# Cross attention and expert layer on one core: score exponentials with an immediate factor instead of a factor read from a tile

## The chip, the cores and the metric

The kernel runs on one core of a Trainium2 chip. The metric is the device time of one execution in microseconds (us); the median of several executions is compared.

## What is computed

Eight batches of 512 tokens, width 512. The first layer is cross attention with 16 heads of 32; the second is an expert layer. Cut to what matters here:

```python
qh = (layernorm(x) @ Wq + bq)   # 16 heads of 32
kh, vh = ctx @ Wk + bk, ctx @ Wv + bv
sim = einsum('bnid,bnjd->bnij', qh, kh) * 32 ** -0.5
sim = where(~attention_mask[:, None, None, :], finfo.min, sim)
attn = softmax(sim, axis=-1)
x = x + (attn @ vh) @ Wo + bo
x = x + experts(layernorm(x))   # 8 experts, each takes its top 512 tokens
```

The mask has one value per batch and key. If a batch had no valid key at all, every score would be the same large negative number and the softmax would be uniform; the kernel must keep that case. With the inputs given, every key is valid.

## The kernel before

**Groups.** The work of attention is cut into 32 groups: a group is one batch and four heads, so a batch is four groups. For a group the kernel projects q and k (`proj`, lines 1888 to 1890, three matmuls per 128 rows of the width, since each float32 operand is split into a rounded part and a rest, called hi and lo). The projections leave PSUM twice: ScalarE writes the hi part with the bias (L1271), VectorE the lo part (L1480). SyncE stores both to memory (`keep_hi`, `keep_lo`) and loads them again as a stack of rows per head (`stack_hi`, `stack_lo`), so that one matmul of 97 or 99 rows gives the exact product of the split numbers, with further rows for the mask and the row maxima. The q weights and the q bias carry the factor -1/sqrt(32), so every score in PSUM has its sign turned.

**Two passes over the scores.** The first pass (`max`, 16 matmuls per group, L1906) has queries on the partitions. VectorE takes the minimum (L1495), which is the negative of the row maximum, and ScalarE forms exp(-(score) + minimum) with its sum (`sum`, L1294). The maxima are turned (`rows`, L1923) and written into the q stack by two small DMAs from GpSimd's queue. The second pass (`score`, 16 matmuls, L1938) has keys on the partitions, with the maximum already subtracted by the extra rows; ScalarE forms the exponential into one of ten buffers `p_ring` (L1306), and `att` (L1950) multiplies it by v. Here the exponential's factor is read from the tile `keep_scale`, one column per batch: -1 where a batch has a valid key, and 0 where it has none, so that all exponentials are 1 there.

**Where the factor comes from.** In the hand-written first steps VectorE computes the mask row (`mask`, L1444), and later (`any`, L1447 to L1451) a block of -1, the maximum of each mask row, and a diagonal of it; TensorE multiplies the two (`scale`, L1854) and VectorE copies the result (L1455).

**Once per batch.** The next batch's x is loaded, its statistics taken (L1399 to L1403), normalised (L1408), turned by TensorE (`turn`, L1848) and split: ScalarE copies the hi part (L1242), VectorE subtracts for the lo part (L1425). The context is split the same way (L1251, L1431), v projected (L899 to L901), and the output projected, added to x, normalised and routed (L1966 to L2000).

**What sets the order.** Up to the first six maxima of group 1 the order is written out in `first_steps`, and PSUM banks are handed out in turn by `take_bank`. From there a planner (`Plan.run`) simulates the five engines with the table `COST`: for each kind of step how long the engine is taken and after how long the result is seen. Each step has a due time `at` in units of groups, from tables of tuned numbers (`LAG`, `K_AT`, `Q_AT`, `MAX_AT`, `SPAN`). Of the steps that could start on an engine within 0.0426 us of the earliest it takes the one with the earliest due time. The order that comes out is the order in which each engine's program is written; banks are given in the same simulation. At run time only semaphores count. After group 31 the kernel chooses the tokens of the experts and runs the expert layer, which the planner doesn't touch.

Line numbers above 1230 and below 1350 are ScalarE's program, 1390 to 1800 VectorE's, above 1840 TensorE's.

## Time and profile before

| | us |
|---|---|
| Median of 3 runs | 1653.18 (1652.41 to 1653.51) |
| Span of the profiled execution | 1648.1 |
| Median less span, what lies around it | 5.1 |

The profiled execution shows a span of 1648.1 us from the first to the last instruction; its own time outside the span isn't recorded, so the 5.1 us are the median less the span. Engines are called PE (TensorE; PEld are its weight loads), ACT (ScalarE), DVE (VectorE), POOL (GpSimd) and SP (SyncE). The page's second part cuts the span into 40 slices of 41.2 us and gives the busy tenths of each:

```profile
PE   7999999999999999999885999999999999999998
DVE  7687978879788797887736688675554555454553
ACT  5899898998989989899863223222222223232321
PEclk9999999999999999999988999999999999999999
```

Attention fills the first 21 slices, the choice of tokens the next one, and the experts the rest.

### The profile page before, as it was taken

The numbers are of one execution on the slowest core, as the hardware profiler recorded it, in microseconds if no ns is written. First come the engines' busy times: TensorE is split into PE (matmuls) and PEld (weight loads), VectorE is DVE, ScalarE is ACT, GpSimd is POOL, SyncE is SP. The second block draws the span as 40 slices with busy tenths as digits, with TensorE's granted clock in tenths as the row PEclk, the third lists the DMA queues.
The fourth block names the chain that finished last, engine by engine and source line by source line (L and its number), as shares of the span: only waits on it lengthen the run. The fifth ranks groups of instructions, "written<-read, shape, count | busy, mean of one in ns | idle before, by whom it ended". The sixth has DMA issues, their size and how long they took to land.

```text
span 1648.1 us, 22236 instructions
## 1 busy us (share of the span) xinstructions
PE 1581.2 (96%) x7826; PEld 1164.5 (71%) x7826; DVE 1118.8 (68%) x1976; ACT 979.2 (59%) x2119; POOL 302.8 (18%) x396
## 2 busy tenths in 40 slices
PE   7999999999999999999885999999999999999998
PEld 5657666676666766667543777888888888888886
DVE  7687978879788797887736688675554555454553
ACT  5899898998989989899863223222222223232321
POOL 6220321302213032130300201002020202020100
PEclk9999999999999999999988999999999999999999
DMA  5543644636446364463601433416253525333340
GB/s 180 178 137 105 204 143 136 187 106 204 142 136 187 106 203 142 138 185 110 205 36 65 129 102 96 142 52 186 77 160 103 160 78 159 103 103 134 99 131 26
DMA packets 131271, 217.26 MB, mean 132 GB/s; under 512 B 17117, under 2 KB 51057, under 8 KB 131161
## 3 DMA queue, kind: packets, MB, share of 16 engines
q1 hardware_dynamic: 114520, 173.23, 33.4%
q0 software_dynamic: 16640, 42.61, 9.9%
q8 instruction: 63, 1.03, 0.3%
q14 instruction: 48, 0.39, 0.1%
HBM read 157.45 MB, written 57.82 MB: 131 GB/s over the span
## 4 chain that ended last, share of the span: by engine, by line
PE 72%; DVE 13%; ACT 9%; DMA 3%; issue 2%; POOL 0%; SPq 0%; ACTq 0%; DVEq 0%; POOLq 0%
PE ps_gen L899 9%; PE ps_gen L900 9%; PE ps_gen L901 9%; PE ps_gen L2107 7%; PE ps_gen L2108 7%; PE ps_gen L2109 7%; PE ps_att L1950 5%; PE ps_gen L1938 4%; PE ps_gen L1906 4%; ACT ps_gen L1294 4%; ACT p_ring L1306 4%; DVE nmax L1495 4%; PE ps_gen L1888 2%; PE ps_gen L1889 1%; PE ps_gen L1890 1%
## 5 line engine op out<-in xcount | busy, mean ns | idle before, releaser
L1495 DVE TENSOR_REDUCE nmax<-ps_gen 128x1 f32<-128x512 f32 x512 | 329.6, 684 | 60.5 <-PE ps_gen L1906 59.8
L1294 ACT ACTIVATE ps_gen<-ps_gen,nmax 128x512 f32<-128x512 f32 x512 | 350.2, 695 | 24.5 <-DVE nmax L1495 24.1
L1306 ACT ACTIVATE p_ring<-ps_gen,keep_scale 128x512 f32<-128x512 f32 x512 | 343.7, 716 | 32.6 <-PE ps_gen L1938 28.7
L1368 ACT ACTIVATE gel<-ps_gen,b_cols 128x512 f32<-128x512 f32 x128 | 88.4, 690 | 446.3 <-PE ps_gen L901 434.1
L1770 DVE TENSOR_TENSOR gel_lo<-gel,gel_hi 128x512 fp32r<-128x512 f32 x126 | 87.3, 693 | 269.3 <-ACT gel_hi L1369 265.0
L899 PE MATMUL ps_gen<-hT_hi,w_hi 128*128 128x512 f32 x504 | 199.2, 395 | 0.0
L2107 PE MATMUL ps_gen<-w_hi,gel_hi 128*128 128x512 f32 x504 | 198.0, 393 | 0.0
L901 PE MATMUL ps_gen<-hT_hi,w_lo 128*128 128x512 f32 x504 | 196.4, 390 | 0.0
L2109 PE MATMUL ps_gen<-w_hi,gel_lo 128*128 128x512 f32 x504 | 196.4, 390 | 0.0
L900 PE MATMUL ps_gen<-hT_lo,w_hi 128*128 128x512 f32 x504 | 196.3, 390 | 0.0
L2108 PE MATMUL ps_gen<-w_lo,gel_hi 128*128 128x512 f32 x504 | 196.2, 389 | 0.0
L1938 PE MATMUL ps_gen<-qst,kst 99*128 99x512 f32 x512 | 192.2, 423 | 3.2 <-ACT p_ring L1306 2.3
L1906 PE MATMUL ps_gen<-kst,qst 97*128 97x512 f32 x512 | 184.3, 415 | 8.1 <-issue 6.0
L1216 POOL DMA_INDIRECT out_x<-y_out,idx x28 | 48.7, 1739 | 508.9 <-ACT y_out L1388 502.5
L1938 PEld LDWEIGHTS ps_gen<-qst,kst 99*128 99x128 f32 x512 | 93.8, 190 | 62.8 <-issue 33.5
L1906 PEld LDWEIGHTS ps_gen<-kst,qst 97*128 97x128 f32 x512 | 96.6, 189 | 58.4 <-issue 26.9
L1950 PE MATMUL ps_att<-p_ring,v_sb 128*32 128x512 f32 x1024 | 127.6, 617 | 4.2 <-ACT p_ring L1306 3.9
L1294 ACT ACTIVATION_READ_ACCUMULATOR ps_gen<-ps_gen,nmax 128x1 f32 x512 | 122.8, 240 | 0.0
L901 PEld LDWEIGHTS ps_gen<-hT_hi,w_lo 128*128 128x128 f32 x504 | 94.6, 188 | 20.2
L2109 PEld LDWEIGHTS ps_gen<-w_hi,gel_lo 128*128 128x128 f32 x504 | 94.6, 188 | 19.7
L2107 PEld LDWEIGHTS ps_gen<-w_hi,gel_hi 128*128 128x128 f32 x504 | 94.8, 188 | 19.3
L899 PEld LDWEIGHTS ps_gen<-hT_hi,w_hi 128*128 128x128 f32 x504 | 94.6, 188 | 19.3 <-issue 0.2
(233 smaller groups left out, 2699.9 us busy)
## 6 DMA issues: line engine op xcount, KB each, us to landing
w_raw<-in_L_ffn_W SPq DMA_DIRECT2D x128, 512.0 KB, 5.2
kst<-qk_rows SPq DMA_DIRECT2D x93, 256.0 KB, 3.9
qst<-qk_rows SPq DMA_DIRECT2D x93, 256.0 KB, 3.7
x_in<-in_x POOLq DMA_DIRECT2D x60, 256.0 KB, 4.0
out_x<-x_in SPq DMA_DIRECT2D x32, 256.0 KB, 2.3
qk_rows<-kT_hi SPq DMA_DIRECT2D x31, 256.0 KB, 2.2
qk_rows<-kT_lo SPq DMA_DIRECT2D x31, 256.0 KB, 3.5
qk_rows<-qT_hi SPq DMA_DIRECT2D x31, 256.0 KB, 2.0
```

Source lines behind the costliest of these rows:

```text
L899: e.matmul(psum, lhsT=wh, rhs=mh, start=(i == 0), stop=False)
L900: e.matmul(psum, lhsT=wh, rhs=ml, start=False, stop=False)
L901: last = e.matmul(psum, lhsT=wl, rhs=mh, start=False, stop=(i == n - 1))
L1294: e.activation(psum[:, :], psum[:, :], ACT.Exp, bias=nmax[g % 2][:, c], scale=-1.0, accum_out=den[g % 2][:, c]).then_inc(drained_sem("max" ...
L1306: e.activation(p_ring[n % NP_][:, :], ps("score", g, kt, h)[:, :], ACT.Exp, scale=keep_scale[:, b:b + 1]).then_inc(drained_sem("score", g, ...
L1495: e.tensor_reduce(nmax[g % 2][:, h * TB + t:h * TB + t + 1], ps("max", g, h, t)[:, :], AX.X, ALU.min).then_inc(s_min, 1)
L1906: e.matmul(ps("max", g, h, t)[:, :], lhsT=qst[k][0:ROWS_MAX, h, t * P:(t + 1) * P], rhs=kst[k][0:ROWS_MAX, h, :], start=True, stop=True).t ...
L1938: e.matmul(ps("score", g, kt, h)[:, :], lhsT=kst[k][0:ROWS_ALL, h, kt * P:(kt + 1) * P], rhs=qst[k][0:ROWS_ALL, h, :], start=True, stop=Tr ...
L1950: last = e.matmul(ps_att[h * DH:(h + 1) * DH, :], lhsT=v_sb[:, kt, (c4 * HG + h) * DH:(c4 * HG + h + 1) * DH], rhs=p_ring[((g * KT + kt) * ...
L2107: e.matmul(ps_y[tt], lhsT=gh, rhs=wh, start=(j == 0), stop=False)
L2108: e.matmul(ps_y[tt], lhsT=gh, rhs=wl, start=False, stop=False)
L2109: return e.matmul(ps_y[tt], lhsT=gl, rhs=wh, start=False, stop=(j == NF - 1))
```

## The change

The exponential of the second pass takes the immediate factor -1. The case of a batch without a valid key is carried by the operands instead: `keep`, 1 or 0 per batch, is multiplied into x as it leaves PSUM after the turn (hi and lo), and into the q bias (`bias_q`, one column per batch and group), so q is zero there; and the mask row of such a batch is multiplied by the batch's own maximum and so becomes zero. The memset, the maximum and the diagonal move into the `mask` step at the head of VectorE's queue, the matmul and the copy of the factors to just ahead of the first turn. The cost table gets the new times for `score` and `turn` on ScalarE and `turn_lo` on VectorE; the due times stay.

```diff
--- before.py
+++ after.py
@@ -283,6 +283,7 @@
     a.add("picks")
     a.stats(0, 0)
     a.add("csplit", 0, 0)
+    a.with_bank("scale")
     for t in range(TB):
         if t + 1 < TB:
             a.add("csplit", 0, t + 1)
@@ -322,7 +323,6 @@
     for t in range(TB):
         a.max_of(0, 0, t)
     a.flush()
-    a.add("any")
     for w, h in (("k", 1), ("q", 2)):
         for i in range(DC):
             a.project(w, 1, i)
@@ -336,7 +336,6 @@
     for t in range(TB):
         a.max_of(0, 3, t)
     a.flush()
-    a.with_bank("scale")
     a.with_bank("v", 0, 1)
     a.max_rows(0)
     a.flush()
@@ -355,12 +354,12 @@
     "pe": {"proj": (0.700, 0.90), "max": (0.235, 0.43), "rows": (0.109, 0.31), "rden": (0.436, 0.63), "score": (0.235, 0.43),
            "att": (1.975, 2.03), "v": (2.78, 2.98), "turn": (0.436, 0.63), "outa": (1.395, 1.60), "osum": (1.650, 1.85),
            "out": (1.395, 1.60), "route": (0.436, 0.63), "logits": (0.405, 0.52), "back": (0.109, 0.31)},
-    "act": {"proj": (0.585, 0.73), "sum": (0.662, 0.82), "rows": (0.174, 0.30), "score": (0.570, 0.72), "osplit": (0.613, 0.79),
-            "csplit": (0.520, 0.66), "turn": (0.477, 0.64), "out": (0.570, 0.70), "logits": (0.157, 0.31), "route": (0.477, 0.64),
+    "act": {"proj": (0.585, 0.73), "sum": (0.662, 0.82), "rows": (0.174, 0.30), "score": (0.477, 0.63), "osplit": (0.613, 0.79),
+            "csplit": (0.520, 0.66), "turn": (0.570, 0.73), "out": (0.570, 0.70), "logits": (0.157, 0.31), "route": (0.477, 0.64),
             "choice_exp": (0.136, 0.26), "wsplit": (0.585, 0.72)},
     "dve": {"proj_lo": (0.658, 0.78), "max": (0.600, 0.72), "rows_lo": (0.313, 0.32), "recip": (0.160, 0.30), "rden": (0.597, 0.72),
             "divide": (0.592, 0.72), "osplit_lo": (0.659, 0.78), "v": (0.570, 0.72), "csplit_lo": (0.600, 0.72),
-            "stats": (1.020, 1.10), "norm": (0.453, 0.57), "turn_lo": (0.598, 0.72), "outa": (0.600, 0.72), "out": (1.750, 1.80),
+            "stats": (1.020, 1.10), "norm": (0.453, 0.57), "turn_lo": (0.660, 0.78), "outa": (0.600, 0.72), "out": (1.750, 1.80),
             "x1_norm": (0.453, 0.57), "route": (0.602, 0.72), "back": (0.300, 0.35), "choice_max": (0.330, 0.41),
             "choice": (0.540, 0.60), "wsplit": (0.660, 0.78), "tables": (0.500, 0.60)},
     "pool": {"rows_lo": (1.050, 3.20), "recip": (0.560, 0.66), "load": (0.550, 4.00), "load_wo": (0.550, 3.30),
@@ -616,7 +615,8 @@
         bs_b = sb(p1, "bs_b", [P, E])
         bias_cols = sb(p1, "bias_cols", [P, 3 * DC])
         half = sb(p1, "half", [P, 1])
-        keep_scale = sb(p1, "keep_scale", [P, B])
+        keep = sb(p1, "keep", [P, B])
+        bias_q = sb(p1, "bias_q", [P, B, DC])
         nmax = [sb(p1, f"nmax{i}", [P, HG * TB]) for i in range(2)]
         den = [sb(p1, f"den{i}", [P, HG * TB]) for i in range(2)]
         rden = sb(p1, "rden", [P, HG * TB])
@@ -625,7 +625,7 @@
         rstd = [sb(p1, f"rstd{i}", [P, 1]) for i in range(NSTAT)]
         rt_max = sb(p1, "rt_max", [P, TB])
         rt_sum = sb(p1, "rt_sum", [P, TB])
-        mask_any = sb(p1, "mask_any", [B, 1])
+        mask_any = sb(p1, "mask_any", [B, 2])
         mask_diag = hnT[0:B, 3, 0:B]
         ones_b = hnT[0:B, 0, :]
         mask_u8 = hnT[0:B, 1, :].bitcast(U8)
@@ -715,6 +715,7 @@
         s_w_hi, s_w_lo = sem("s_w_hi"), sem("s_w_lo")
         s_picks = sem("s_picks")
         s_mask, s_mask_store, s_any = sem("s_mask"), sem("s_mask_store"), sem("s_any")
+        s_bias_q = sem("s_bias_q")
         s_proj_hi = {w: sem(f"s_proj_hi_{w}") for w in "qk"}
         s_kept_hi, s_kept_lo = {w: sem(f"s_kept_hi_{w}") for w in "qk"}, {w: sem(f"s_kept_lo_{w}") for w in "qk"}
         s_stack_hi = {w: [sem(f"s_stack_hi_{w}{i}") for i in range(NST)] for w in "qk"}
@@ -842,6 +843,10 @@
 
         def stack_of(w, g):
             return (qst if w == "q" else kst)[g % NST]
+
+        def bias_of(w, g):
+            b, c4 = divmod(g, GB)
+            return bias_q[:, b, c4:c4 + 1] if w == "q" else bias_cols[:, DC + c4:DC + c4 + 1]
 
         def kept(w, g, part):
             return qk_rows["qk".index(w), g % 2, part]
@@ -1239,8 +1244,9 @@
                     on.wait_ge(*full("turn", b, t))
                     if b > 0:
                         on.wait_ge(*full("proj", "q", b * GB - 1))
+                    on.wait_ge(*drained("scale"))
                     e.activation(xT[0][:, :, t * P:(t + 1) * P], ps("turn", b, t)[:, :].rearrange("p (c t) -> p c t", c=DC),
-                                 ACT.Copy).then_inc(s_turn_hi, 1)
+                                 ACT.Copy, scale=keep[:, b:b + 1]).then_inc(s_turn_hi, 1)
 
                 elif kind == "csplit":
                     b, c = at
@@ -1260,8 +1266,7 @@
 
                 elif kind == "proj" and at[2] == DC - 1:
                     w, g, _ = at
-                    n = ("q", "k").index(w) * DC + g % GB
-                    on.wait_ge(*drained("bias"))
+                    on.wait_ge(*(drained("bias") if w == "k" else (s_bias_q, 1)))
                     on.wait_ge(*full("proj", w, g))
                     if g == 1:
                         on.wait_ge(*full("pick", w, HG - 1))
@@ -1269,7 +1274,7 @@
                         on.wait_ge(s_kept_hi[w], 16 * (g - 1))
                         on.wait_ge(*drained("proj", w, g - 1))
                     e.activation(qk[w, "hi"][:, :], ps("proj", w, g)[:, :], ACT.Identity,
-                                 bias=bias_cols[:, n:n + 1]).then_inc(s_proj_hi[w], 1)
+                                 bias=bias_of(w, g)).then_inc(s_proj_hi[w], 1)
 
                 elif kind == "pick" and at[1] % 2 == 0:
                     w, h = at
@@ -1296,15 +1301,13 @@
 
                 elif kind == "score":
                     g, kt, h = at
-                    b = g // GB
                     n = (g * KT + kt) * HG + h
-                    on.wait_ge(*drained("scale"))
                     on.wait_ge(s_w_lo, W_NO["o"])
                     on.wait_ge(*full("score", g, kt, h))
                     if n >= NP_:
                         on.wait_ge(s_av, (n - NP_) // (PAIR * HG) + 1)
                     e.activation(p_ring[n % NP_][:, :], ps("score", g, kt, h)[:, :], ACT.Exp,
-                                 scale=keep_scale[:, b:b + 1]).then_inc(drained_sem("score", g, kt, h), 1)
+                                 scale=-1.0).then_inc(drained_sem("score", g, kt, h), 1)
 
                 elif kind == "osplit":
                     g, = at
@@ -1422,8 +1425,9 @@
                     hi, lo = xT
                     cols = slice(t * P, (t + 1) * P)
                     on.wait_ge(s_turn_hi, b * TB + t + 1)
-                    e.tensor_tensor(lo[:, :, cols], ps("turn", b, t)[:, :].rearrange("p (c t) -> p c t", c=DC),
-                                    raw(hi[:, :, cols]), ALU.subtract).then_inc(drained_sem("turn", b, t), 1)
+                    on.wait_ge(*drained("scale"))
+                    e.scalar_tensor_tensor(lo[:, :, cols], ps("turn", b, t)[:, :].rearrange("p (c t) -> p c t", c=DC), keep[:, b:b + 1],
+                                           raw(hi[:, :, cols]), ALU.mult, ALU.subtract).then_inc(drained_sem("turn", b, t), 1)
 
                 elif kind == "csplit_lo":
                     b, c = at
@@ -1441,23 +1445,27 @@
 
                 elif kind == "mask":
                     on.wait_ge(s_mask_in, 16)
-                    e.tensor_scalar(mask_neg, mask_u8, 1.0, -MASKED, ALU.subtract, ALU.mult).then_inc(s_mask, 1)
-
-                elif kind == "any":
-                    e.memset(ones_b, -1.0).then_inc(s_any, 1)
-                    e.reduce_max(mask_any[:, :], mask_u8, AX.X).then_inc(s_any, 1)
+                    e.memset(ones_b, 1.0).then_inc(s_any, 1)
+                    e.reduce_max(mask_any[:, 0:1], mask_u8, AX.X).then_inc(s_any, 1)
                     on.wait_ge(s_any, 2)
+                    e.tensor_scalar(mask_any[:, 1:2], mask_any[:, 0:1], -MASKED, None, ALU.mult).then_inc(s_any, 1)
                     on.wait_ge(s_ident, 2)
                     e.tensor_scalar(mask_diag, ident[0:B, 0:B], mask_any[:, 0:1], None, ALU.mult).then_inc(s_any, 1)
+                    on.wait_ge(s_any, 3)
+                    e.tensor_scalar(mask_neg, mask_u8, 1.0, mask_any[:, 1:2], ALU.subtract, ALU.mult).then_inc(s_mask, 1)
 
                 elif kind == "scale":
                     on.wait_ge(*full("scale"))
-                    e.tensor_copy(keep_scale[:, :], ps("scale")[:, 0:B]).then_inc(drained_sem("scale"), 1)
+                    e.tensor_copy(keep[:, :], ps("scale")[:, 0:B]).then_inc(drained_sem("scale"), 1)
 
                 elif kind == "bias":
                     on.wait_ge(*full("bias"))
                     e.tensor_copy(bias_cols[:, DC:3 * DC], ps("bias")[:, DC:3 * DC])
                     e.tensor_scalar(bias_cols[:, 0:DC], ps("bias")[:, 0:DC], -SCALE, None, ALU.mult).then_inc(drained_sem("bias"), 1)
+                    on.wait_ge(*drained("bias"))
+                    on.wait_ge(*drained("scale"))
+                    e.tensor_tensor(bias_q[:, :, :], bias_cols[:, 0:DC].rearrange("p (b c) -> p b c", b=1).to_broadcast([P, B, DC]),
+                                    keep[:, :].rearrange("p (b c) -> p b c", c=1).to_broadcast([P, B, DC]), ALU.mult).then_inc(s_bias_q, 1)
 
                 elif kind == "wsplit":
                     w, c = at
@@ -1470,14 +1478,13 @@
 
                 elif kind == "proj_lo":
                     w, g = at
-                    n = ("q", "k").index(w) * DC + g % GB
                     on.wait_ge(s_proj_hi[w], g + 1)
-                    on.wait_ge(*drained("bias"))
+                    on.wait_ge(*(drained("bias") if w == "k" else (s_bias_q, 1)))
                     if g == 1:
                         on.wait_ge(*full("pick", w, HG - 1))
                     if g > 1:
                         on.wait_ge(s_kept_lo[w], 16 * (g - 1))
-                    e.scalar_tensor_tensor(qk[w, "lo"][:, :], ps("proj", w, g)[:, :], bias_cols[:, n:n + 1],
+                    e.scalar_tensor_tensor(qk[w, "lo"][:, :], ps("proj", w, g)[:, :], bias_of(w, g),
                                            raw(qk[w, "hi"][:, :]), ALU.add, ALU.subtract).then_inc(drained_sem("proj", w, g), 1)
 
                 elif kind == "pick" and at[1] % 2 == 1:
@@ -1850,7 +1857,7 @@
 
                 elif kind == "scale":
                     on.wait_ge(*free("scale"))
-                    on.wait_ge(s_any, 3)
+                    on.wait_ge(s_any, 4)
                     e.matmul(ps("scale")[:, 0:B], lhsT=ones_b, rhs=mask_diag, start=True, stop=True).then_inc(full_sem("scale"), 1)
 
                 elif kind == "bias":
```

## Rows read from the trace of the kernel before

**Rows 1.** The page, part 1: busy us, share of the span, instructions.
```profile
PE 1581.2 (96%) x7826; PEld 1164.5 (71%) x7826; DVE 1118.8 (68%) x1976; ACT 979.2 (59%) x2119; POOL 302.8 (18%) x396
```

**Rows 2.** Busy time by group of attention: length, engines' busy time, granted clock, DMA.
```profile
77.50:106.40 28.90, 26.06 (x127) 13.97 (x127) 24.84 (x50) 28.21 (x67) 13.22 (x17) 0.95 0.64 189
...
153.90:180.80 26.90, 26.90 (x153) 18.80 (x152) 23.54 (x46) 21.44 (x49) 4.67 (x8) 1.00 0.59 186
180.80:208.60 27.80, 26.78 (x149) 17.09 (x148) 27.25 (x63) 27.24 (x65) 10.82 (x18) 1.00 0.71 201
208.60:232.30 23.70, 23.48 (x119) 15.60 (x116) 18.18 (x31) 22.21 (x53) 6.45 (x7) 1.00 0.45 134
...
826.60:850.20 23.60, 19.60 (x93) 11.47 (x89) 12.77 (x21) 18.36 (x42) 1.58 (x3) 0.86 0.05 20
```

**Rows 3.** Chain of waits, 180.8 to 208.6: start, length, what (first, last).
```profile
180.60 0.60 DVE hnT L1542
...
208.05 0.61 DVE nmax L1495
```

**Rows 4.** Chain of waits, 208.6 to 260 us.
```profile
208.68 0.78 ACT ps_gen L1294 x2
...
219.30 1.16 ACT p_ring L1306 x2
...
226.84 0.66 PE ps_gen L1930 x4
```

**Rows 5.** Waits 150 to 790 us: who, after whom, us, times, longest.
```profile
PEld ps_att L1950 <- ACT p_ring L1306: 5.5, 17, 0.4
...
PEld ps_gen L1938 <- ACT p_ring L1306: 3.7, 13, 0.4
PEld ps_gen L1906 <- ACT ps_gen L1294: 3.2, 12, 0.3
PEld ps_gen L1966 <- ACT ps_gen L1294: 2.9, 6, 0.5
...
PEld ps_gen L1930 <- ACT ps_gen L1294: 2.6, 6, 0.5
...
PE ps_gen L1906 <- issue: 1.1, 3, 0.7
PE ps_gen L1966 <- ACT ps_gen L1294: 1.0, 6, 0.2
```

**Rows 6.** Instructions by line and shape: count, busy us, mean ns, idle before.
```profile
L1306 ACT ACTIVATE p_ring<-ps_gen,keep_scale 128x512 f32<-128x512 f32 x512 | 343.7, 716 | 32.6 <-PE ps_gen L1938 28.7 <-PE ps_att L1950 3.7
...
L1242 ACT ACTIVATE xT_hi<-ps_gen 128x512 fp32r<-128x512 f32 x32 | 19.2, 615 | 2.6 <-PE ps_gen L1848 2.4
...
L1480 DVE SCALAR_TENSOR_TENSOR qT_lo<-ps_gen,bias_cols,qT_hi 128x512 fp32r<-128x512 f32 x32 | 24.0, 749 | 28.2 <-ACT qT_hi L1271 27.9
...
L1425 DVE TENSOR_TENSOR xT_lo<-ps_gen,xT_hi 128x512 fp32r<-128x512 f32 x32 | 20.9, 683 | 0.0
```

**Rows 7.** Chain of waits, 0 to 110 us.
```profile
54.68 1.74 ACT p_ring L1306 x3
...
63.78 5.58 DMA qk_rows<-qT_hi
...
98.24 0.97 ACT xT_hi L1242 x2
```

**Rows 8.** Chain of waits, 800 to 880 us: the last four scores.
```profile
863.95 2.43 ACT p_ring L1306 x4
```

**Rows 9.** Timeline of the start: start, length, engine, line, [idle before <-releaser].
```profile
8.28 0.69 DVE L1399 BATCH_NORM_STATS2 stat<-x_in 128x6 f32<-128x512 f32 x1 [0.63 <-DMA x_in<-in_x]
...
31.64 2.58 DVE L1451 TENSOR_SCALAR hnT<-ident,mask_any 8x8 f32<-8x8 f32 x1
...
32.38 1.81 POOL L1097 MEMSET qst<- 32x2048 f32 x1
...
41.92 0.50 PE L899 MATMUL ps_gen<-wv_hi,cT_hi 128*128 128x512 f32 x1 [0.28 <-ACT ps_gen L1294]
```

## The prediction, made before the changed kernel ran

> **What bounds the kernel now.** I read the page's first section, then the busy time of each engine over single attention groups, then the chain of waits, and last the waits by engine. Over the whole execution TensorE is busy 96% of the span and ScalarE 59% [rows 1]. That average hides three stages: a start of some 52 us, attention up to about 870 us, and the experts, which the change doesn't touch. The question is who limits attention.
>
> Attention runs in batches of four groups, and the groups are not alike [rows 2]. In the group from 153.9 us TensorE is busy for all of its 26.9 us. In the next one, from 180.8, VectorE is busy for 27.25 of 27.8 us and ScalarE for 27.24, while TensorE loses a microsecond: this is where the next batch is normalised and turned. After it TensorE is again at 23.48 of 23.7 us. The first batch (77.5 to 106.4) and the last (826.6 to 850.2) are looser for TensorE, and its granted clock dips to 0.95 and 0.86 there.
>
> The chain of waits says the same in another way. From 180.6 to 208.7 us it stays on VectorE alone [rows 3]. Then it lies on ScalarE from 208.68 to 226.8 us, and from 226.84 on TensorE [rows 4]. So ScalarE, whose work gets cheaper, holds the end for some 18 us of each batch, with TensorE close behind it. Last, the waits from 150 to 790 us: TensorE's weight loads stood idle after ScalarE for 5.5 + 3.7 + 3.2 + 2.9 + 2.6 = 17.9 us, and its matmuls for 1.0 us [rows 5]. That stretch has six full batches.
>
> **The change, part by part.** The profiled execution has a span of 1648.1 us; the median of the runs is 1653.18, so 5.1 us lie around the span. I leave those alone and give the result as a median.
>
> *A score exponential.* It reads the factor from a tile now, and takes 716 ns; a copy from PSUM with an immediate factor takes 615 ns [rows 6]. What counts is the step from one to the next in the chain: 1.16 us for two scores, so 0.58 [rows 4], against 0.97 for two turns, 0.485 [rows 7]. I take 0.095 us off each of 512 scores, 48.6 us of ScalarE's time. Nothing in the trace shows an exponential without any operand from a tile; the price lies between 0 and the 101 ns of the durations, and I take the one nearest, the copy. Per batch that is 64 x 0.095 = 6.1 us, and most of it is worth nothing, since ScalarE isn't last there.
>
> *What of it reaches the end, between the first and the last batch.* The chain's ScalarE stretch holds 14 scores: 14 x 0.095 = 1.33 us, in six batches 8.0 us. But TensorE is idle only 0.2 us in that group, so as soon as ScalarE is faster it is the bound. The lower end is what TensorE's matmuls waited for ScalarE, 1.0 us; the upper end adds the weight loads, 18.9 us. I take 6, the chain's value cut a little because TensorE is so near.
>
> *The turns.* Four times a batch ScalarE's copy of the turned x gets a factor from a tile (+0.095 each) and VectorE's subtraction becomes the three-operand form with a factor from a tile: 683 becomes 749 ns [rows 6], +0.066. The four subtractions lie in the group where the chain is VectorE throughout [rows 3], so nothing covers them: 6 x 4 x 0.066 = +1.6 us. The four copies lie beside the relief of 16 scores there.
>
> *First batch.* The chain from 54.7 to 99.2 us carries 18 scores and three turns [rows 7]: -18 x 0.095 + 3 x 0.095 = -1.4 us. **Last batches.** From 797 us on it carries 14 scores, the last four in one row of 2.43 us [rows 8]: -1.3 us.
>
> *The start.* New on VectorE, ahead of the first statistics, are a memset, a maximum over the mask rows, a tiny product and the diagonal. They, and the copy of the factors, are covered by the wait for x, which still ends at 8.28 after 0.63 us of idleness [rows 9]; without that cover they would cost some 1.3 us. The step at risk is the diagonal: in the old place it took 2.58 us for 8x8 elements, and ended at 34.22, when GpSimd's memset ended at 34.19 [rows 9]. GpSimd is filling the picking matrices where the step goes. I take +0.2 from a range of 0 to 2.6. The Trainium skill (SBUF — State Buffer, section "Who interferes with whom") says that VectorE and GpSimd share one pair of ports as an exclusive lock, and the second to issue stands until the first is done. By it the diagonal and the mask row would both stand behind GpSimd's fill, and the start would cost about 1 us more than my sum has. The trace agrees for the old place.
>
> The product of bias and factors adds a small VectorE instruction (about 0.2 us with its wait) on the path to the first projections, and one dearer copy with three dearer subtractions there adds 0.09 + 3 x 0.066 = 0.3. In return the old step is gone from between the first projections (0 to 2.58 us, mostly under the wait for the k rows), and a bank is no longer taken before the v tiles, where TensorE stood 0.28 us for ScalarE [rows 9]. I take -0.5. The start is +0.2 + 0.2 + 0.3 - 0.5 = +0.2 us. The matmul for the factors only moves; no DMA is added, and in the start the SyncE queue keeps its order: it issues the mask's store behind all the first loads, when the row has long been there.
>
> *The sum:* -6.0 + 1.6 - 1.4 - 1.3 + 0.2 = -6.9 us; 1653.2 - 6.9 = 1646.3, and I give 1646. A difference under 0.2% (3.3 us) can't be told from none by a measurement of this kernel.
>
> **The planner.** Orders on all queues and the banks are computed from the cost table, so three new costs reshuffle them from batch 0 on, with due times that stay. This is a mechanism of its own that the sum can't contain; it makes the two rivals at the ends.
>
> **The rivals.** (1) *VectorE and TensorE hold the pace.* The gain behind 208 us vanishes because TensorE was ready to be last, and only the first and last batches gain: 1.6 - 1.4 - 1.3 + 0.2 = -0.9, 1652.3. For it speaks TensorE's 99% in that group; against it the waits behind ScalarE.
> (2) *Much more.* A less loaded ScalarE lets the planner close all waits behind it: -18.9 + 1.6 - 1.4 - 1.3 + 0.2 = -19.8, 1633.4. For it: every dip of the granted clock (0.95, 0.86) stands where TensorE waited, so they would go as well. Against it: weight loads' waits are partly hidden behind matmuls.
> (3) *Slower: the q and k rows come late.* Rows are stored, and loaded again as a stack, and the first maximum of the next group waits for them. In the first batch the store alone took 5.58 us and stood in the chain [rows 7]. In the steady part this is just in time: three waits, 1.1 us, the longest 0.7 [rows 5]. If the reshuffle puts a projection behind scores that now come ready earlier, each of 24 groups may wait 0.7 us: +16.8 - 6.9 = +9.9, 1663. It decides against the forecast from (6.9 + 3.3) / 24 = 0.43 us a group.
> (4) *The exponential isn't cheaper without the tile.* Then only the additions are left: +1.6 + 0.3 + 0.2 = +2.1, 1655.3. Nothing speaks for it but that no row shows such an exponential.
>
> **How the numbers follow.** Forecast 0.45; (1) 0.20; (2) 0.13; (3) 0.18; (4) 0.04. Faster: 0.45 + 0.13 = 0.58. Same: 0.20 + 0.04 = 0.24. Slower: 0.18. The range goes from close to rival 2 to where a mild form of rival 3 ends, 1634 to 1657.
>
> **What would show it.** Scores at about 615 ns and stepping 0.485 us; turns at 716 and 749 ns; the group with the turns still 27.8 us or a little more, its chain VectorE; the group after it about 1 us shorter, TensorE's waits on ScalarE down from 18.9 to under 10 us; the first statistics for x tile 2 still near 8.3 us. I would be wrong if the four groups kept their lengths, if scores kept 716 ns, or if first maxima waited on landings.

## The result, and the profile after

The changed kernel takes 1671.13 us (median of 4 runs, 1668.95 to 1675.18), the kernel before 1653.35 (4 runs): a ratio of 1.0106, 95% interval 1.0087 to 1.0125. It is 17.8 us slower where 7 us less had been forecast, and lies outside the range. The span of the profiled execution grew from 1648.1 to 1667.1 us.

First what went as foreseen. The page, part 1, and the groups by line and shape [rows 1, 6 before]:

```profile
PE 1589.0 (95%) x7826; PEld 1171.2 (70%) x7826; DVE 1118.8 (67%) x1978; ACT 943.8 (57%) x2119; POOL 298.1 (18%) x396
...
L1309 ACT ACTIVATE p_ring<-ps_gen 128x512 f32<-128x512 f32 x512 | 289.7, 611 | 45.9 <-PE ps_gen L1945 38.6 <-PE ps_att L1957 3.3
...
L1429 DVE SCALAR_TENSOR_TENSOR xT_lo<-ps_gen,keep,xT_hi 128x512 fp32r<-128x512 f32 x32 | 22.3, 739 | 0.0
L1248 ACT ACTIVATE xT_hi<-ps_gen,keep 128x512 fp32r<-128x512 f32 x32 | 20.3, 674 | 12.3 <-PE ps_gen L1855 12.3
```

A score exponential takes 611 instead of 716 ns, and ScalarE is busy for 35.4 us less (943.8 instead of 979.2). The sums of the first pass, which did not change, are 21 ns shorter too (674 instead of 695). The turns take 739 (683 before) and 674 ns (615 before). From one score to the next, the chain of waits has 0.485 us, as forecast (0.58 before, [rows 4]):

```profile
264.74 0.97 ACT p_ring L1309 x2
```

Yet TensorE, with the same 7826 matmuls, is busy for 7.8 us more.

The time of single groups, in the columns of [rows 2] (a window begins with the first score of its group):

```profile
157.80:184.70 26.90, 26.90 (x155) 18.53 (x153) 23.10 (x47) 20.68 (x49) 5.23 (x9) 1.00 0.61 186
184.70:214.30 29.60, 27.99 (x145) 18.40 (x144) 26.66 (x60) 26.40 (x64) 8.93 (x17) 0.88 0.65 175
214.30:239.80 25.50, 24.75 (x122) 16.77 (x121) 20.31 (x34) 23.22 (x59) 7.06 (x8) 1.00 0.58 172
239.80:263.90 24.10, 23.91 (x120) 16.52 (x119) 14.23 (x25) 20.28 (x51) 1.58 (x3) 1.00 0.18 56
...
291.80:319.30 27.50, 25.64 (x146) 16.86 (x145) 26.18 (x60) 25.90 (x64) 8.95 (x17) 1.00 0.68 192
```

The group with the turns takes 29.6 us in one batch and 27.5 in the next, and so on alternately; the granted clock is 0.88 in the long one. The group after it, which the forecast had a microsecond shorter than its 23.7 us, takes 25.5. Only in the first of the four is an engine, TensorE, busy throughout. In the next two TensorE stands idle for 1.6 and 0.75 us, and no other engine fills the group either. The waits of TensorE's matmuls and weight loads from 150 to 790 us (columns of [rows 5]):

```profile
PE ps_gen L1913 <- ACT ps_gen L1299: 8.9, 9, 1.4
PE ps_gen L1973 <- ACT ps_gen L1299: 4.5, 6, 0.8
PE ps_gen L1988 <- DVE x_in L1411: 2.5, 3, 1.0
...
PEld ps_gen L1913 <- ACT ps_gen L1299: 13.3, 17, 1.6
PEld ps_gen L1945 <- ACT p_ring L1309: 9.1, 32, 0.4
```

TensorE waits for ScalarE longer than before, although each score left ScalarE a tenth of a microsecond of room: the matmuls for 8.9 + 4.5 us behind the sums, where they had 1.0 [rows 5]. The timeline around the first of these waits (start, length, engine, line, in brackets the idle time before and its releaser):

```profile
185.44 0.59 ACT L1309 ACTIVATE p_ring<-ps_gen 128x512 f32<-128x512 f32 x1
...
186.02 0.66 ACT L1299 ACTIVATE ps_gen<-ps_gen,nmax 128x512 f32<-128x512 f32 x1
...
186.70 1.14 ACT L1257 ACTIVATE cT_hi<-x_in 128x512 fp32r<-128x512 f32 x2
...
187.74 0.65 ACT L1299 ACTIVATE ps_gen<-ps_gen,nmax 128x512 f32<-128x512 f32 x1
...
188.56 0.50 PE L1913 MATMUL ps_gen<-kst,qst 97*128 97x512 f32 x1 [1.38 <-ACT ps_gen L1299]
```

Two copies of the next context (L1257) stand ahead of a sum in ScalarE's queue, and a maximum waits for the bank that this sum frees. The copies are no dearer than before (639 ns on average, 655 before); they stand elsewhere. A little later the granted clock falls. Two windows of the same group, columns as above:

```profile
184.70:190.00 5.30, 3.92 (x23) 2.39 (x22) 4.50 (x10) 5.24 (x13) 2.19 (x4) 1.00 0.47 157
190.00:196.80 6.80, 6.57 (x22) 4.13 (x23) 5.88 (x13) 5.89 (x16) 1.07 (x2) 0.50 0.73 218
```

TensorE was busy for 3.92 of 5.3 us with a clock of 1.00, and then for 6.8 us the granted clock is 0.50, 1.2 GHz instead of 2.4. Such stretches stand at 190.0, 401.7 and 613.3 us, in every second batch; before there was none between 150 and 790 us.

### The profile page after: what moved, and what is told of

Read it like the earlier page. It is cut to its first block, busy times and chain, and to the rows that moved or that the text cites. A ratio compares the mean times of both kernels' runs of the same rounds, so it can differ in the third digit from the quotient of the medians.

```text
span 1667.1 us, 22244 instructions
## 1 busy us (share of the span) xinstructions
PE 1589.0 (95%) x7826; PEld 1171.2 (70%) x7826; DVE 1118.8 (67%) x1978; ACT 943.8 (57%) x2119; POOL 298.1 (18%) x396
## 3 DMA queue, kind: packets, MB, share of 16 engines
q8 instruction: 63, 1.03, 0.3%
## 4 chain that ended last, share of the span: by engine, by line
PE 73%; DVE 12%; ACT 8%; DMA 4%; issue 2%; POOL 0%; SPq 0%; DVEq 0%; POOLq 0%; ACTq 0%
PE ps_gen L904 8%; PE ps_gen L906 8%; PE ps_gen L905 8%; PE ps_gen L2114 7%; PE ps_gen L2116 7%; PE ps_gen L2115 7%; PE ps_att L1957 5%; PE ps_gen L1945 5%; PE ps_gen L1913 4%; ACT ps_gen L1299 4%; DVE nmax L1502 3%; ACT p_ring L1309 2%; PE ps_gen L1973 2%; PE ps_gen L1895 1%; PE ps_gen L1896 1%
## 5 line engine op out<-in xcount | busy, mean ns | idle before, releaser
L1299 ACT ACTIVATE ps_gen<-ps_gen,nmax 128x512 f32<-128x512 f32 x512 | 342.9, 674 | 44.9 <-DVE nmax L1502 42.7
L1309 ACT ACTIVATE p_ring<-ps_gen 128x512 f32<-128x512 f32 x512 | 289.7, 611 | 45.9 <-PE ps_gen L1945 38.6
L1913 PE MATMUL ps_gen<-kst,qst 97*128 97x512 f32 x512 | 179.1, 419 | 17.5 <-ACT ps_gen L1299 10.3
L1299 ACT ACTIVATION_READ_ACCUMULATOR ps_gen<-ps_gen,nmax 128x1 f32 x512 | 112.1, 219 | 0.0
```

The lines of the kernel that those rows point to most:

```text
L1299: e.activation(psum[:, :], psum[:, :], ACT.Exp, bias=nmax[g % 2][:, c], scale=-1.0, accum_out=den[g % 2][:, c]).then_inc(drained_sem("max" ...
L1309: e.activation(p_ring[n % NP_][:, :], ps("score", g, kt, h)[:, :], ACT.Exp, scale=-1.0).then_inc(drained_sem("score", g, kt, h), 1)
L1913: e.matmul(ps("max", g, h, t)[:, :], lhsT=qst[k][0:ROWS_MAX, h, t * P:(t + 1) * P], rhs=kst[k][0:ROWS_MAX, h, :], start=True, stop=True).t ...
```

## The experiments

**Theory A**: the sum over the instructions is right, and the loss is the order of the queues, which the planner computes from the three changed costs. **Rival B**: the order is no worse than the old one, and the changed instructions cost more than counted (the turns on VectorE's path, the copy of the factors, the start). A second rival came with the results: the order is bad because a certain entry of the table is wrong, and a truer one would mend it.

**Old costs, all changed instructions.**

```diff
-    "act": ... "score": (0.477,0.63) ... "turn": (0.570,0.73)
+    "act": ... "score": (0.570,0.72) ... "turn": (0.477,0.64)
-    "dve": ... "turn_lo": (0.660, 0.78)
+    "dve": ... "turn_lo": (0.598, 0.72)
```

> The changed kernel with the three old entries of the cost table, so that all queues keep the order of the kernel before, and only the instructions and the start are new. Theory A (the new order is the loss, the instructions gain): about 1646 us, my forecast's sum, 1640 to 1651. Rival B (the dearer turns and the new start cost more than cheaper exponentials give, in any order): 1660 to 1672, near the changed kernel. Rival C (neither counts for much, the half clock stretches are chance): near 1653 with or without them.

Measured: 1646.13 us (5 runs), ratio 0.9960 (0.9946 to 0.9974). The forecast's sum was 1646.3. The planner writes every planned step of this kernel in the same place as in the kernel before. The groups, in the columns of [rows 2]:

```profile
153.00:179.90 26.90, 26.90 (x153) 18.86 (x152) 23.76 (x46) 20.52 (x49) 4.38 (x8) 1.00 0.57 186
179.90:207.90 28.00, 26.48 (x149) 17.14 (x148) 27.17 (x62) 26.79 (x64) 10.92 (x18) 1.00 0.69 206
207.90:230.80 22.90, 22.90 (x118) 15.49 (x115) 17.90 (x31) 21.05 (x53) 6.42 (x7) 1.00 0.39 130
230.80:255.10 24.30, 24.30 (x124) 16.93 (x123) 14.98 (x25) 22.70 (x56) 1.60 (x3) 1.00 0.33 90
```

The group with the turns takes 28.0 us (27.8 before), the next one 22.9 (23.7), and TensorE is busy in the whole of it. Of the waits from 150 to 790 us, the largest that is left behind ScalarE, and the longest of a matmul:

```profile
PEld ps_gen L1973 <- ACT ps_gen L1299: 2.4, 6, 0.4
...
PE ps_gen L1913 <- issue: 0.8, 2, 0.6
```

No stretch of lower clock stands between 150 and 790 us. Theory A holds: between this kernel and the changed one lie 25 us, and only the order differs, with the PSUM banks that go with it.

**New costs, all old instructions** (the reverse edit in the kernel before).

> The kernel before, with the three new entries of the cost table and nothing else: the changed kernel's order with the old instructions. Theory A: slower than the changed kernel, since the exponentials keep their 716 ns: 1672 to 1685 us. Rival B: near 1653, since none of the new instructions is there. Rival C: 1650 to 1660.

Measured: 1687.36 us, 1.0202 (1.0181 to 1.0223). This is theory A again, 2 us above its range, and no rival's. Both kernels have the same planned order. It costs the old instructions 33 us, the new ones 25.

**Which entry is it?** The changed kernel with the two turn entries of the table old, and with the score entry old:

```diff
-"turn": (0.570,0.73) ... "turn_lo": (0.660, 0.78)      # first
+"turn": (0.477,0.64) ... "turn_lo": (0.598, 0.72)
-"score": (0.477,0.63)                                  # second
+"score": (0.570,0.72)
```

> The changed kernel with the old entries for the turns alone, and the new one for the score. If the score's entry makes the bad order, the time stays at 1668 to 1675 us. If the turns' entries make it, the time falls to about 1646 to 1653.

> The changed kernel with the old entry for the score and the new ones for the turns: the reverse of the run in which the turns' entries were old. Sharp theory A: the plan's own end is 832.6 us, worse than with all three entries new (824.0), so about 1660 to 1680. Rival D: the turns' entries are four small steps in a batch, so near the changed kernel in the old order: 1645 to 1650.

Measured: 1674.61 us, 1.0125 (1.0099 to 1.0150), and 1683.41, 1.0172 (1.0149 to 1.0196). Each time is near the upper end of what was expected or above it (1668 to 1675, 1660 to 1680). Either change alone, the score entry's or the turn entries', is enough to lose the gain, and together (1671.1) they cost no more than either alone. These are not two effects that add up.

**Is it the size of the entry?** The kernel before, its score entry smaller by 10 ns and nothing else; and the changed kernel with a score entry of 0.460.

```diff
-"score": (0.570, 0.72)      # kernel before
+"score": (0.560, 0.713)
-"score": (0.477, 0.63)      # changed kernel
+"score": (0.460, 0.613)
```

> The kernel before with one number changed: the planner's entry for the score is 0.560 and 0.713 us in place of 0.570 and 0.72, ten nanoseconds less. Theory A in its sharp form (the due times fit one cost table exactly, and any other entry scatters the order): the plan's own end goes from 820.6 to 834.5 us, so the time should rise by about 14 us or more, to 1667 to 1690. Rival D (it was the size of the correction that mattered, scores that really come much earlier overtaking the maxima): ten nanoseconds change next to nothing, 1650 to 1657 us.

> The changed kernel with the score's entry at 0.460 and 0.613 us, 17 ns under what it takes. The plan's own end is 822.5 us, its batch 103.2, against 824.0 and 103.6 for the changed kernel. If the plan's end ranks orders, 1666 to 1671 us. If the loss comes from orders that are tight by wrong costs, this one, with an entry that is too low, should be no better than the changed kernel: 1671 or above.

Measured: 1706.03 us, 1.0310 (1.0277 to 1.0344), and 1667.52, 1.0074 (1.0048 to 1.0099). Ten nanoseconds in one entry cost 50 us, 16 more than the upper end expected. The entry that is 17 ns too low gave 1667.5 us beside 1671.1 with the measured one, so a truer entry doesn't mend the order, and the second rival is out. What waits there, from 160 to 820 us:

```profile
PE ps_gen L1906 <- issue: 16.5, 11, 2.9
```

These are the first maxima that wait for rows to land: rival 3 of the prediction, in a kernel whose table differs by one digit. In the changed kernel this wait does not appear; with the entry of 0.460 it comes to 3.8 us in five waits.

**The immediate factor alone**, in the kernel before, its order and its table kept (it leaves out the case of a batch without a valid key):

```diff
-ACT.Exp, scale=keep_scale[:, b:b + 1]
+ACT.Exp, scale=-1.0
```

> The kernel before, old order, whose score exponential takes the immediate factor -1, and nothing else is changed: the case of a batch without a valid key isn't handled in this kernel. It gives the exponentials' gain without the dearer turns and the new start. Theory A: 1.5 to 3 us faster than the changed kernel in the old order, about 1643 to 1645 us. Rival B: also clearly under 1653, but 15 us or more under the changed kernel in the old order. If the exponential were no cheaper for the path: 1653.

**Plain turns** in the old order (the changed kernel, old costs, `keep` not multiplied into x; the same case is left out):

```diff
-ACT.Copy, scale=keep[:, b:b + 1]
+ACT.Copy
-e.scalar_tensor_tensor(lo, ps, keep[:, b:b + 1], raw(hi), ALU.mult, ALU.subtract)
+e.tensor_tensor(lo, ps, raw(hi), ALU.subtract)
```

> The changed kernel in the old order, with plain turns: ScalarE's copy without the factor and VectorE's two-operand subtraction, so the case of a batch without a valid key isn't handled in this kernel. My forecast's term for the turns, 24 x 0.066 us plus 0.3 at the start: 1.9 us less than with the dear turns, about 1644 us. If ScalarE covers them or VectorE has room there: no difference, 1646.

Measured: 1648.33 us, 0.9967 (0.9957 to 0.9976), and 1646.71, 0.9960 (0.9946 to 0.9974). In the first the exponential takes this much (groups by line, shape kept apart):

```profile
L1306 ACT ACTIVATE p_ring<-ps_gen 128x512 f32<-128x512 f32 x512 | 291.5, 602 | 45.7 <-PE ps_gen L1938 38.5 <-PE ps_att L1950 4.0
```

The immediate factor brings 5.6 us by itself. The 1643 to 1645 us expected of it were missed: it is no faster than all changes together in the same order (1646.1). With the dearer turns taken away nothing more is gained either, 1646.7. In both profiled executions one first maximum comes late:

```profile
513.52 0.47 PE L1906 MATMUL ps_gen<-kst,qst 97*128 97x512 f32 x1 [1.15 <-issue]
```

```profile
512.58 0.47 PE L1913 MATMUL ps_gen<-kst,qst 97*128 97x512 f32 x1 [1.23 <-issue]
```

The first line is from the kernel before with the immediate factor, the second from the plain turns. Each makes its batch about a microsecond longer (103.05 and 103.17 us beside 102.1 to 102.2), and the clock did not fall behind it.

**New due times for the new table.** All due times were searched again, from two starts, for the earliest end in the planner's own reckoning: 796.3 and 803.4 us, against 824.0 for the changed kernel and 820.6 for the one before.

```diff
-K_AT = ((0.17737, 0.32917), (-0.06676, 0.27306), (0.03391, 0.12332), (-0.36248, 0.0798))
+K_AT = ((0.35915, 0.39022), (-0.13871, 0.11178), (-0.45119, 0.37669), (-0.05366, 0.45826))
...
```

> The changed kernel with its new cost entries and due times sought anew for them, by random steps that keep whatever made the plan's own end earlier: it is 796.3 us in place of 824.0, the batch 99.6 in place of 103.6. If the plan's end is what the chip follows (theory A: due times and costs have to fit each other), about 28 us less than the changed kernel: 1640 to 1648 us. If the plan's model leaves out what decides on the chip, an order pressed hard against the model gains less than half of that: 1655 to 1670.

> The same with another start of the search, the plan's end at 803.4 us, its batch 100.4. If the chip follows the plan: 7 us later than the other one, 1647 to 1655 us. If the model leaves out what decides, their order on the chip may be the reverse, both above 1655.

Measured: 1661.48 us (10 runs, from 1654.6 to 1668.4, a wider spread than the other kernels'), 1.0048 (1.0029 to 1.0067), and 1712.62, 1.0360 (1.0335 to 1.0385). The chip doesn't follow the plan's end: a gain under half of the 28 us for the first, a loss of 41 us against the changed kernel for the second. The waits of the second, from 160 to 820 us:

```profile
PE ps_gen L1975 <- DVE x_in L1398: 29.4, 6, 5.1
PE ps_gen L1932 <- DMA qst<-by_row: 15.2, 10, 2.6
```

In the second, TensorE waits 29.4 us for normalised x whose slot an output store still holds (L1398), and 15.2 us for the rows of maxima. So a plan that is shorter by the table isn't a faster kernel, and these waits are for transfers: that is the theory tested last.

**One wait by hand.** The changed kernel's order, with six steps moved after the planner has run: in batches 2 to 7 the sum stands ahead of the two copies of the context (first), or the sum and the two scores behind it (second).

```diff
+    act = a.order["act"]
+    for b in range(2, B):
+        i = act.index(("csplit", b, 0))
+        act[i:i + 3] = [act[i + 2], act[i], act[i + 1]]      # first
+        act[i:i + 5] = act[i + 2:i + 5] + act[i:i + 2]       # second
```

> The changed kernel and its order, but in batches 2 to 7 ScalarE's queue has one sum ahead of two copies of the context instead of behind them (six places, nothing else moves). In the changed kernel TensorE waits there 1.38 us, for the bank that this sum frees, and its clock falls to 1.2 GHz for 6.8 us in every second batch. Theory A, the order of single steps costs through such pauses and the clock falls because of them: the pause shrinks by two copies (1.14 us) to about 0.3, the half-clock stretches of 190, 402 and 613 us go, and the time is 1671 - 20.5/2 - 3 to 6 x 1.0 = 1655 to 1659. Theory B, the clock falls for another reason: pauses shrink but the stretches stay, 1665 to 1668. Theory C, the pause only moves (the context loads or the copies are late next, VectorE is last in this group): 1671, the group keeps its 29.6 us.

> As the last one, but the two copies of the context stand behind the sum and behind the two scores that follow it (batches 2 to 7), about as in the order of before. With the sum alone ahead of them, TensorE's 1.38 us were split into 0.34 us behind the sum and 1.03 us behind a score, the copies being late either way, and the clock fell in every batch instead of every second. Theory A, ScalarE's queue at this place is the cause and the copies can wait: both waits go, no half-clock stretch is left between 150 and 790 us, the turn group takes 27.0 instead of 27.5 to 29.7 us, and the time is 1671 - 6 x 1.0 - 3 x 2.2 = 1655 to 1660. Theory B, the wait moves on once more, to VectorE's lo parts, the loads of x behind them and the normalised x: a wait of 1 us or more of TensorE for x_in or hnT appears, and the time is 1670 to 1685.

Measured: 1681.18 us, 1.0167 (1.0149 to 1.0184), and 1689.00, 1.0210 (1.0193 to 1.0227): each slower than the last, the first above all three of its theories, the second 4 us above its theory B, whose sign, a wait for hnT, is there. The same place in the first, in a later batch, and then in the second (timelines):

```profile
293.45 0.49 PE L1918 MATMUL ps_gen<-kst,qst 97*128 97x512 f32 x1 [0.34 <-ACT ps_gen L1304]
294.98 0.49 PE L1950 MATMUL ps_gen<-qst,kst 99*128 99x512 f32 x1 [1.03 <-ACT p_ring L1314]
```

```profile
299.41 0.65 PE L2004 MATMUL ps_gen<-hnT,ws_sb 128*32 128x128 f32 x8 [2.43 <-DVE hnT L1554]
```

The 1.38 us turned into 0.34 + 1.03, behind the score that the copies now delay, and then into 2.43 us, because VectorE's queue has the lo parts of the same copies ahead of a copy (hnT) that TensorE needs.

**Both queues together.** As the second, and VectorE's two lo parts also stand behind what TensorE waited for:

```diff
+        dve = a.order["dve"]
+        i = dve.index(("csplit_lo", b, 0))
+        dve[i:i + 5] = dve[i + 2:i + 5] + dve[i:i + 2]
```

> As the last one (ScalarE's two context copies behind a sum and two scores), and VectorE's two lo parts of them stand behind a turned row block (hnT), a logits block and a maximum instead of ahead of them. In the last kernel TensorE waited 2.43 us for hnT behind these lo parts. Theory A, the two queues have to be moved together and then the wait is gone: no matmul waits longer than 0.8 us in the turn group, the stretches of half clock there vanish, the turn group takes 27 to 28 us and the time is 1655 to 1662. Theory B, the copies themselves are needed early, because the loads of x wait for them (the slots are shared): the statistics and the normalised x of the same group come later, TensorE waits for x_in, and the time stays at 1675 to 1690.

Measured: 1672.23 us, 1.0128 (1.0109 to 1.0147). The wait for hnT is gone (waits 150 to 790 us), and one behind a score is back:

```profile
PE ps_gen L1954 <- ACT p_ring L1318: 6.0, 6, 1.0
...
PE ps_gen L2008 <- DVE hnT L1558: 1.3, 5, 0.3
```

Against the second kernel some 15 us came back, against the changed one nothing. Neither theory had it quite: the two queues do belong together, but the pause of a microsecond returned at the next score. By hand this order wasn't mended.

**Due times searched against late landings.** The changed kernel, all due times searched again from two starts, this time for the mean end over the table's landing times and three sets of longer ones. The edit has the form of the retuned kernels' above.

> The changed kernel with all due times searched anew, as the two retuned kernels, but for the mean end over four sets of landing times of the transfers (the table's, and stores, reloads, row writes and loads 0.6 to 1.2 us longer, in part and all together). The first retuned kernels ended at 796 and 803 us by the table but lost 1.5 to 11 us per batch on the chip to waits for landings. This plan ends at 803 by the table and at 814 with all transfers longer; the order of before gives 821 and 852 in the same reckoning. Theory A, what the earlier plans missed were landings: about 102 us per batch at most, 1635 to 1646. Theory B, pauses of TensorE from other causes and the clock that falls after them decide, which no due time knows of: above 1650, with stretches of half clock between 150 and 790 us.

> As the last one, from another start of the search: 801 us by the table, 816 with all transfers longer. The same expectations: theory A 1635 to 1646, theory B above 1650. Two plans of nearly equal end also show how far apart such plans fall on the chip: the two earlier ones fell 51 us apart; if landings were the reason these should lie within 10 us of each other.

Measured: 1636.37 us (5 runs), 0.9905 (0.9885 to 0.9924), and 1645.78 (6 runs), 0.9955 (0.9940 to 0.9970). All that TensorE's matmuls still waited for in the first, from 150 to 790 us:

```profile
PE ps_gen L1994 <- ACT ps_gen L1286: 3.0, 6, 0.5
PE ps_gen L1932 <- DMA qst<-by_row: 2.1, 3, 0.8
PE ps_gen L1882 <- ACT ps_gen L1286: 2.0, 6, 0.3
```

No stretch of lower clock stands there in the first. It is faster than both kernels of this case, and than the old order with the new instructions; a batch takes 101.6 us on the chip and 100.6 by its plan, where the earlier retuned ones took 103.8 against 99.8, and 111.5 against 100.4. The second is just inside theory A's range, but shows theory B's signs: 103.5 us against 100.2, with three short stretches at 1.2 GHz and a pause of 1.7 us behind a sum. The two lie 9 us apart, within the 10 expected. In the first only 2.1 us of waits for landings are left, where the second of the earlier plans had 15.2 + 29.4. So late landings explain much of that plan's loss, and not all of what plans miss. That searching against them is what makes a plan better isn't shown by two plans of each kind, since each search also moved everything else. Both plans end later by the table than the first retuned one (803 and 801 against 796 us), and are 25 and 16 us faster on the chip. How much the old instructions would gain with such due times wasn't tried.

All kernels side by side. "Plan" is the planner's own end; "batch" is a sixth of the time from the first score of group 4 to that of group 28; "half" is the time at 1.2 GHz in between. The plans of the three orders moved by hand end at 824.0 before the move.

| kernel | instructions | table: score, turns | plan | batch, us | half, us | median, us |
|---|---|---|---|---|---|---|
| before | old | old, old | 820.6 | 102.9 | 0 | 1653.4 |
| e5_before_immediate | factor only | old, old | 820.6 | 102.3 | 0 | 1648.3 |
| e1_old_costs | new | old, old | 820.6 | 102.2 | 0 | 1646.1 |
| e8_plain_turns | new, plain turns | old, old | 820.6 | 102.5 | 0 | 1646.7 |
| after | new | new, new | 824.0 | 105.8 | 20 | 1671.1 |
| e2_new_costs_only | old | new, new | 824.0 | 109.2 | 41 | 1687.4 |
| e4_turn_costs_old | new | new, old | 823.8 | 106.6 | 24 | 1674.6 |
| e3_score_cost_old | new | old, new | 832.6 | 107.4 | 7 | 1683.4 |
| e6_score_cost_560 | old | 0.560, old | 834.5 | 111.8 | 27 | 1706.0 |
| e9_score_cost_460 | new | 0.460, new | 822.5 | 104.9 | 7 | 1667.5 |
| e7_retuned_a | new | new, new; due times | 796.3 | 103.8 | 3 | 1661.5 |
| e7_retuned_b | new | new, new; due times | 803.4 | 111.5 | 31 | 1712.6 |
| e10_sum_first | new | new, new; by hand | - | 108.4 | 48 | 1681.2 |
| e11_copies_later | new | new, new; by hand | - | 109.5 | 58 | 1689.0 |
| e12_both_later | new | new, new; by hand | - | 106.4 | 24 | 1672.2 |
| e13_robust_a | new | new, new; due times | 802.9 | 101.6 | 0 | 1636.4 |
| e13_robust_b | new | new, new; due times | 801.1 | 103.5 | 10 | 1645.8 |

As long as the due times stay, the plan's end puts the kernels with the new instructions in their measured order but for 0.2 us (820.6, 822.5, 823.8, 824.0, 832.6), though not to scale: 3.4 us of plan were 25 on the chip. Between different due times it doesn't rank them.

## Why the prediction was wrong

**The step that failed** is the paragraph on the planner, and with it rival 3's chance of 0.18. I wrote that three new costs reshuffle every queue and that the sum can't contain this, and then gave the sum 0.45 all the same, as if the new order would on average be as good as the old. So the sum has this term at nothing, and it measured 25.0 us with the new instructions (1671.1 against 1646.1) and 33.4 with the old ones. The old order goes with due times tuned for its table; of five other tables here (after, e3, e4, e6, e9) each gave a longer batch and a slower kernel, by 12 to 50 us against the kernel before. Seen from there the likeliest case was a loss, of a size that no row of before could bound.

**Where the 25 us went**, between e1_old_costs and the changed kernel (spans 1642.0 and 1667.1): up to the first score of group 4, 4.8 us (153.0 to 157.8); the six batches behind it 21.5 us; the end -1.2. Of the 4.8 us, 1.7 stand ahead of the first score of all (51.2 and 52.9 us), in steps whose order is the same in both: there the second tile of x landed at 5.57 and at 7.33 us. One batch of each without any stretch of lower clock, the sums over its four groups, first of the changed kernel (263.9 to 368.9 us), then of e1 (255.3 to 357.5):

```profile
sum 105.00, PE 101.63 PEld 68.42 DVE 83.89 ACT 90.07 POOL 22.86; mean PE 25.41 PEld 17.10 DVE 20.97 ACT 22.52 POOL 5.72
```

```profile
sum 102.20, PE 100.66 PEld 68.54 DVE 83.63 ACT 91.11 POOL 22.95; mean PE 25.16 PEld 17.14 DVE 20.91 ACT 22.78 POOL 5.74
```

VectorE and ScalarE do the same work in both. TensorE stands idle for 3.4 us instead of 1.5 and is busy 1.0 us longer; that is 2.8 us a batch, of which the planner's own plan has 1.3 (102.3 to 103.6). The three batches without a stretch take 104.9 us on average (104.0 to 105.6), which makes 6 x 2.7 = 16 us. The other 5.5 lie in the three batches with a stretch at 1.2 GHz: they take 106.7 us, and their turn group 29.6 to 29.8 instead of 27.5. That the order is the cause of all this is shown by e1 and e2; that the single wait behind the context copies is, is not: moving it by hand made things worse.

**Rival 3** had the sign, not the mechanism. Against e1 the batch grew by 0.9 us per group, twice the 0.43 from which it decides, but from pauses behind sums and from stretches at the lower clock. The first maxima waited long for landings only in e6 (16.5 us); e3, e5, e8 and e9 have 2.1 to 3.8 us of such waits, the changed kernel none. My last sentence, that I would be wrong if they did, named the wrong sign to look for.

**The sum came true** in the order for which it was made: 1646.3 forecast, 1646.13 measured in e1. That it did so to a fifth of a microsecond is luck. Term by term: the exponential, 0.105 us less by its duration (0.095 taken), also with no operand from a tile at all, so rival 4 is out. *Six batches*, -6.0 + 1.6 = -4.4 forecast: 102.9 to 102.2 us each, -4.2. *Start and first batch*, -1.2: the first score of group 4 at 153.9 and 153.0 us, -0.9. *Last batches*, -1.3: what is left of the 6.1 us of span, -1.0. *Waits on ScalarE*, 18.9 to under 10: TensorE's weight loads had 6.2 us left in e1. *The turn group*: 27.8 to 28.0, chain on VectorE up to 205.0 us. *The group after it*: 23.6 to 23.0, where about 1 us had been forecast, with the chain on TensorE throughout; so rival 1's mechanism took part of the relief. By their times rivals 1 and 2 are out in that order too.

**The relief and the turns** were both taken too large, and the errors nearly cancel. I charged the turns 1.6 us because four subtractions stand in VectorE's chain. The medians are too coarse for that (1646.7 with plain turns beside 1646.1), but the groups show it: the turn group takes 27.96 to 28.00 us in e1 and 27.82 to 27.90 in the three batches of e8 without a long pause, the whole batch 102.17 to 102.26 and 102.07 to 102.18. That is about 0.1 us a batch, 0.6 in six. The exponentials by themselves, in the batches of e5 without a long pause, brought 0.75 us a batch (102.92 to 102.17 on average), 4.5 in six where I took 6.

**The start** was sized well, and its risk not met. The timeline of the changed kernel, columns as in [rows 9]:

```profile
1.53 1.79 POOL L1079 MEMSET qst<- 128x2048 f32 x1
...
2.44 0.62 DVE L1449 TENSOR_REDUCE mask_any<-hnT 8x1 f32<-8x512 uint8 x1
...
3.09 0.14 DVE L1451 TENSOR_SCALAR mask_any<-mask_any 8x1 f32<-8x1 f32 x1
3.16 0.21 DVE L1453 TENSOR_SCALAR hnT<-ident,mask_any 8x8 f32<-8x8 f32 x1
3.29 0.47 DVE L1455 TENSOR_SCALAR att_n<-hnT,mask_any 8x512 f32<-8x512 uint8 x1
...
3.73 0.69 DVE L1402 BATCH_NORM_STATS2 stat<-x_in 128x6 f32<-128x512 f32 x1
```

The diagonal takes 0.21 us instead of 2.58, and the first statistics start at 3.73 us. The next ones wait for x until 7.35 us, where x tile 1 had let them start at 5.50 in the kernel before. That moves those for x tile 2 to 9.42 us (8.28 before), away from the 8.3 that I gave as a sign; but it isn't the new steps, for in e1, with the same start, they stand at 5.59 and 7.80 us. This tile lands at 5.5 to 7.3 us, different in each profiled execution.

Why the same instruction took 2.58 us in the old place can be read from the traces side by side. It reached VectorE at 3.16 us, when GpSimd's memset had only 0.16 us left. In e1_old_costs it came a little earlier, and in e6_score_cost_560, which has it in the old place, in the middle of another memset:

```profile
1.53 1.79 POOL L1079 MEMSET qst<- 128x2048 f32 x1
3.08 0.27 DVE L1453 TENSOR_SCALAR hnT<-ident,mask_any 8x8 f32<-8x8 f32 x1
```

```profile
30.07 1.80 POOL L1094 MEMSET kst<- 32x2048 f32 x1
31.46 0.43 DVE L1451 TENSOR_SCALAR hnT<-ident,mask_any 8x8 f32<-8x8 f32 x1
```

In the four traces with the old place it took 2.58, 2.26, 2.26 and 0.43 us and ended 0.02 us behind the end of a memset each time, in the kernel before at 34.22 beside 34.19 [rows 9]. In the thirteen with the new place it ends 0.02 us behind the memset where it started by 3.13 us (0.22 to 0.28 us), and takes 0.21 us where it started later. So it stands until the memset is done, and costs 0.21 us otherwise. This is the lock that the Trainium skill describes (SBUF — State Buffer, "Who interferes with whom"), and these traces agree with it. The microsecond that the prediction worked out by it did not come, because so little of the memset was left.

## What to carry to other kernels

Where a planner writes the order, a corrected entry of its cost table is a change of the order and has to be measured alone: keep the old table to see what the instructions bring, and put the new table under the old instructions to see what the order does. Here due times tuned for one table didn't carry over to another, not even by 10 ns. Search them again, and try landings later than the table's as well, since the plan with the earliest end by exact times was 25 us slower here than one that was 7 us longer on paper. Measure every plan, for two of nearly equal end fell 51 us apart. A wait in a queue is seldom mended by moving one step: the copies moved past one wait came back as the next one, on the same engine or on its neighbour.

## What the runs showed of the hardware

The granted clock of TensorE fell from 2.4 to 1.2 GHz in the middle of a kernel that keeps it busy for 95% of the span, for stretches of 3.4, 6.8 and 10.2 us. Most of them came within 4 us of a pause of TensorE of 1.0 us or more, but no rule comes out of these runs:

- 1.38 us were followed by a stretch in every second batch of the changed kernel and in every batch of e2, and 0.34 + 1.03 us at the same place in every batch.
- 1.15 us in e5, 1.23 in e8, and 1.45 and 1.30 in e9 were followed by none.
- In e6 a stretch of 6.8 us began at 253.2 us, though in the 8 us ahead of it no pause was longer than 0.21 us; in the second robust plan one began at 502.2, behind nothing longer than 0.49.

```profile
245.20:253.20 8.00, 7.57 (x29) 5.07 (x27) 5.22 (x8) 6.92 (x16) 0.00 (x0) 1.00 0.59 164
253.20:260.00 6.80, 6.78 (x23) 2.35 (x23) 1.95 (x3) 4.78 (x13) 0.00 (x0) 0.50 0.01 2
```

Before, e1 and the first robust plan had no pause over 0.82 us and no stretch between 150 and 790 us. A stretch of 6.8 us in the changed kernel cost 2.2 us in its group, not 3.4; VectorE is busy there for 26.7 of the 29.6 us.

A tiny tensor_scalar on VectorE (8x8 elements, 0.21 us by itself) stood until GpSimd's memset was done, up to 2.58 us; the maximum over the mask rows (0.62 us) ran beside the same memset without standing.
